# A four-layer transformer kernel, third layer: the mixing step one batch behind instead of two, the gates in one group, unread matmuls in front and beside the first batch

## The reference, cut to what matters

```python
x = x + _L2_xattn_ref(_layernorm(x), ctx, ctx, ...)      # mLSTM
x = x + _L2_ffn_ref(_layernorm(x), W_r, W_k, W_v, mu_r, mu_k)

# mLSTM, per batch and head
gate_input = concat([q, k, v])                # q: normalised x; k, v: ctx
ig, fg = gate_input @ ig_kernel + ig_bias, gate_input @ fg_kernel + fg_bias
cums = cumsum(log_sigmoid(fg))
log_D = cums_i - cums_j + ig_j  (j <= i);  m = max_j log_D;  D = exp(log_D - m)
C = (qh @ kh.T / 8) * D
n = maximum(abs(C.sum(-1)), exp(-m))
h = (C / (n + 1e-6)) @ vh;  h = layernorm(h) * outnorm_weight

# feed-forward
x_prev = x shifted by one token
xr, xk = mu_r * x + (1 - mu_r) * x_prev,  mu_k * x + (1 - mu_k) * x_prev
out = sigmoid(xr @ W_r.T) * (square(relu(xk @ W_k.T)) @ W_v.T)
```

## Time and profile before

| what | us |
| --- | --- |
| median of 3 runs | 1605.3 (1603.09 to 1617.99) |
| the profiled execution, its own time | 1609.19 |
| its span, first to last instruction | 1607.6 |
| the third layer: first DMA issue to last addition | 850.29 to 1091.33 |
| first window's `spread` | 882.15 |
| TensorE busy over the span | 1328.7 (83%) |
| VectorE, ScalarE, GpSimd busy over the span | 808.6, 484.4, 494.1 |

### The profile page before, as it was taken

How to read it: one execution, slowest core, us unless ns; L and a number is a source line. 1 busy time by engine, 2 the same in 40 slices (tenths; PEclk the granted TensorE clock), 3 DMA queues, 4 the chain that set the end, 5 groups by cost and what they waited for, 6 DMA issues and landing times. The chain is left out here.

```text
span 1607.6 us, 30539 instructions
## 1 busy us (share of the span) xinstructions
PE 1328.7 (83%) x9980; PEld 1067.6 (66%) x9980; DVE 808.6 (50%) x2539; ACT 484.4 (30%) x1095; POOL 494.1 (31%) x481
## 2 busy tenths in 40 slices
PE   5988899958888887988974899876889888899991
PEld 4766788945555556887874778754555556788881
DVE  6786334445667643332543455753555655333333
ACT  3554011115554430110111334523455443111010
POOL 1245422231323325223122455542222423211110
PEclk9999899979999988999995557987999999899996
DMA  9001343221013005544433000000000301333216
GB/s 302 1 29 42 125 141 122 70 76 33 29 34 117 29 15 178 171 137 132 133 96 115 14 1 1 1 1 20 14 8 22 105 23 41 111 122 122 82 43 219
DMA packets 87027, 123.58 MB, mean 77 GB/s; under 512 B 11425, under 2 KB 61601, under 8 KB 86657
## 3 DMA queue, kind: packets, MB, share of 16 engines
q1 hardware_dynamic: 49744, 56.10, 11.4%
q10 hardware_dynamic: 25824, 34.10, 6.8%
q0 software_dynamic: 11344, 31.92, 5.5%
HBM read 83.96 MB, written 38.13 MB: 76 GB/s over the span
## 5 line engine op out<-in xcount | busy, mean ns | idle before, releaser
L1243 PEld LDWEIGHTS bank<-f_xT,f_up 128*128 128x128 f32 x2144 | 259.8, 195 | 8.4 <-DVE f_xT L1127 3.1
L1243 PE MATMUL bank<-f_xT,f_up 128*128 128x128 f32 x2144 | 261.0, 278 | 2.1 <-DVE f_xT L1127 2.1
L375 DVE TENSOR_REDUCE mha_nmax<-bank 128x2 f32<-128x512 f32 x256 | 170.3, 687 | 162.4 <-PE bank L496 121.0
L1252 PE MATMUL bank<-f_down,f_hT 128*128 128x256 f32 x832 | 202.2, 386 | 16.7 <-DVE f_hT L1161 16.7
L496 PE MATMUL bank<-l_took,mha_q 32*128 32x256 f32 x1024 | 155.7, 424 | 60.6 <-DVE mha_nmax L375 44.8
L281 ACT ACTIVATE l_took<-bank 128x512 f32<-128x512 f32 x256 | 139.3, 598 | 159.2 <-PE bank L504 140.8
L1252 PEld LDWEIGHTS bank<-f_down,f_hT 128*128 128x128 f32 x832 | 151.7, 192 | 40.3 <-issue 23.0
L496 PEld LDWEIGHTS bank<-l_took,mha_q 32*128 32x128 f32 x1024 | 94.0, 195 | 103.0 <-DVE mha_nmax L375 63.9
L504 PE MATMUL bank<-l_took 32*128 32x256 f32 x1024 | 152.1, 415 | 2.2 <-DVE l_took L384 2.0
L1017 POOL DMA_INDIRECT yout<-f_y,f_to x66 | 63.7, 964 | 287.6 <-DVE f_y L1185 165.9
L1059 ACT ACTIVATE f_hT<-bank,f_b 128x128 f32<-128x128 f32 x148 | 46.4, 364 | 319.2 <-PE bank L1243 319.2
(11 more groups left out here) (287 smaller groups left out, 2441.8 us busy)
## 6 DMA issues: line engine op xcount, KB each, us to landing
f_up<-in_W ACTq DMA_DIRECT2D x26, 512.0 KB, 5.1
f_xt<-rows SPq DMA_DIRECT2D x88, 132.0 KB, 2.1
f_down<-in_W ACTq DMA_DIRECT2D x20, 512.0 KB, 6.1
f_xt<-rows SPq DMA_DIRECT2D x20, 264.0 KB, 2.8
ring<-yout SPq DMA_DIRECT2D x8, 512.0 KB, 4.2
mha_ctxT<-in_ctxT SPq DMA_DIRECT2D x16, 256.0 KB, 2.8
l_took<-yout SPq DMA_DIRECT2D x16, 256.0 KB, 5.5
f_up<-in_W SPq DMA_DIRECT2D x6, 512.0 KB, 7.5
```

What stands on the lines that cost most here:

```text
L375: vector.tensor_reduce(nmax[:, p, :, at], ps_s[n % 2][:, :].rearrange("p (k s) -> p k s", s=S), AX.X, ALU.min).then_inc(max_ready, 1)
L1243: ins = pe.matmul(into, up[q][i][:, c, m * P:(m + 1) * P], xT[:, c, :], start=c == 0, stop=c == DC - 1)
L1252: ins = pe.matmul(ps_y[:, 0:D], hT[:, m, :], down[q][:, m, :], start=m == 0, stop=m == HC - 1)
```

## The change

The mixing chain of a batch now runs wholly in the window after its mLSTM step (LAG = 1), so the loop has 9 windows. `project_k` no longer shares its stretch with `gates`, which are a group of eight at the place where `project_k` stood, ordered by tile of tokens; `turn_f` moves between the values of heads 1 and 2, and the three projections follow the values of heads 2 and 3, with `sum_up` and `turn_g` between them. They write other banks (ps_s[0], ps_s[1], ps_q[0] instead of ps_x, ps_s[0], ps_s[1]). The normalisation `f_normalize` goes from GpSimd to VectorE; GpSimd keeps the root. On VectorE `f_mean_and_var` stands first in the window and `mix` behind the weighing of heads 2 and 3. On ScalarE `f_turned` stands before `softened`, and `squared_relu` and `receptance` behind `squares`. TensorE gets 20 unread matmuls at the start of the layer, and in the first window, which has no mixing work, 4 in the place of each projection.

```diff
+    LAG = 1
-            def f_normalize(b):
+            def f_root(b):
                 pool.wait_ge(f_var_ready, b + 1)
                 pool.tensor_tensor(f_rstd[:, b, :], f_var_eps[:, b, :], G.mhalf(TPB), ALU.pow).then_inc(f_rstd_ready, 1)
-                pool.wait_ge(f_rstd_ready, b + 1)
-                after(pool, fT_done, b)
-                for i in range(TPB):
-                    ins = pool.tensor_scalar(fxn[:, i, :], X[:, TPB * b + i, :], f_moments[:, b, i, 0:1],
-                                             f_rstd[:, b, i:i + 1], ALU.subtract, ALU.mult)
-                ins.then_inc(fxn_ready, 1)
...
+                if w_ >= LAG:
+                    f_turned(w_ - LAG)
                 if more:
                     softened(w_ + 1)
-                if w_ >= 2:
-                    receptance(w_ - 2)
                 if now:
                     squares(w_)
-                if 0 < w_ <= B:
-                    f_turned(w_ - 1)
+                if w_ >= LAG:
+                    squared_relu(w_ - LAG)
+                    receptance(w_ - LAG)
...
+            def f_normalize(b):
+                vector.wait_ge(f_rstd_ready, b + 1)
+                after(vector, fT_done, b)
+                for i in range(TPB):
+                    ins = vector.tensor_scalar(fxn[:, i, :], X[:, TPB * b + i, :], f_moments[:, b, i, 0:1],
+                                             f_rstd[:, b, i:i + 1], ALU.subtract, ALU.mult)
+                ins.then_inc(fxn_ready, 1)
...
+            def fill(w_, n):
+                pe.wait_ge(xnT_ready, min(w_ + 2, B))
+                keep_busy(pe, G, ps_x, n)
...
+            keep_busy(pe, G, ps_s[0], 20)
             centre(0)
             turn_x(0)
...
-            for w_ in range(B + 2):
+            for w_ in range(B + LAG):
...
-                if w_ >= 2:
-                    project_k(w_ - 2, w_ + 1 if more else None)
-                elif more:
+                if more:
                     gates(w_ + 1)
...
+                if w_ >= LAG:
+                    turn_f(w_ - LAG)
                 if now:
                     values(w_, 2)
                     values(w_, 3)
+                if w_ >= LAG:
+                    project_k(w_ - LAG)
+                else:
+                    fill(w_, 4)
+                if more:
+                    sum_up(w_ + 1)
+                if w_ >= LAG:
+                    project_r(w_ - LAG)
+                else:
+                    fill(w_, 4)
                 if more:
                     turn_g(w_ + 1)
-                if w_ >= 2:
-                    project_v(w_ - 2)
+                if w_ >= LAG:
+                    project_v(w_ - LAG)
+                else:
+                    fill(w_, 4)
                 if more:
                     turn_m(w_ + 1)
-                if 0 < w_ <= B:
-                    turn_f(w_ - 1)
                 if w_ + 2 < B:
                     turn_x(w_ + 2)
```

More of the change, by code:

```diff
@@ L2149, in _ @@
             vector.wait_ge(w_in, 16 * 4)
-            for w_ in range(B + 2):
+            for w_ in range(B + LAG):
                 now, more = w_ < B, w_ + 1 < B
+                if w_ >= LAG:
+                    f_mean_and_var(w_ - LAG)
                 if now:
@@ L2162, in _ @@
                     mean_and_var(w_ + 2)
+                if w_ + 3 < B:
+                    z_mean_and_var(w_ + 3)
                 if now:
@@ L2208, in turn_x, with gates @@
                 after(pe, xnT_ready, b)
[L2209 to L2210 removed]
+                after(pe, fT_ready, b - 1 - LAG)
                 turn(xn[:, b % 2, :, :]).then_inc(xT_done, 1)
[L2213 to L2220 removed]
+            def gates(b):
                 pe.wait_ge(xnT_ready, b + 1)
@@ L2223, in await_gates @@
                 after(pe, top_ready, b)
-            def gates(b):
-                await_gates(b)
-                for n in range(2 * TPB * DC):
-                    ins = gate(b, n)
+                for k in range(TPB):
+                    for i, source in ((1, ctxT[:, b, :, :]), (0, xnT[:, b % 2, :, :])):
+                        for c in range(DC):
+                            ins = pe.matmul(ps_g[:, 2 * HEADS * k:2 * HEADS * (k + 1)], source[:, c, k * P:(k + 1) * P],
+                                            gates_w[:, i, c, :], start=i == 1 and c == 0, stop=i == 0 and c == DC - 1)
                 ins.then_inc(gates_done, 1)
@@ L2286, in values, with project_k @@
                 ins.then_inc(pv_done, 1)
+            def fill(w_, n):
+                pe.wait_ge(xnT_ready, min(w_ + 2, B))
+                keep_busy(pe, G, ps_x, n)
             def turn_f(b):
                 pe.wait_ge(fxn_ready, b + 1)
[L2290 removed]
+                pe.wait_ge(xnT_ready, min(b + 2 + LAG, B))
                 after(pe, fT_ready, b)
+                turn(fxn).then_inc(fT_done, 1)
+            def project_k(b):
+                pe.wait_ge(k_mixed, b + 1)
+                pe.wait_ge(decay_ready, HEADS * min(b + 1 + LAG, B))
                 after(pe, relu_s, b)
[L2293 to L2311 removed]
+                for m in range(DC):
+                    for c in range(DC):
+                        ins = pe.matmul(ps_s[0][:, m * S:(m + 1) * S], w[:, 1, c, m * P:(m + 1) * P], mixed[:, 1, c, :],
+                                        start=c == 0, stop=c == DC - 1)
+                ins.then_inc(k_done, 1)
             def project(to, source, i):
@@ L2364, in _ @@
                     values(w_, 1)
-                if w_ >= 2:
-                    project_r(w_ - 2)
-                if more:
-                    sum_up(w_ + 1)
+                if w_ >= LAG:
+                    turn_f(w_ - LAG)
                 if now:
```

76 lines of the change are left out of this document (23 added, 53 removed).

## The result

The changed kernel takes 1596.84 us (median of 20 runs, 1580.58 to 1608.01), the kernel before 1611.68 us beside it (20 runs, 1603.09 to 1629.07). The ratio is 0.9913 with a 95% interval of 0.9889 to 0.9937: faster by about 15 us, a little under the 1% (16 us) that the prediction called the least that can be told from no change; a second comparison, with 0.9931, bears it out. The forecast was 1618 us, that is a little slower, and its range of 1582 to 1652 holds the result; the direction was wrong.

A forecast was written before the change was run, and what follows sets the result against it. TensorE was taken to fill the loop's windows, its clock worth more than any wait. Start -1, first window +4, full windows +15 and end -5 gave +13 on 1609.19, or 1618 us on the median's scale, range 1582 to 1652.

The forecast's parts named there:

- case (a): Clock falls near the gates and rises at the projections in each window; 1618 us, about 1600 to 1638; chance 0.52.
- The price of a full window: Full loop windows: 26.3 us each, mean of full-clock and low-clock prices; 158 for six, +15 against 142.8.
- The walk at full clock: A full window followed along TensorE from spread: 20.4 us, bounds 19.7 and 21.2, against 19.3 before.
- The mean of half and half: Full windows priced as the mean of 20.4 us at full clock and 32.1 at low clock: 26.3 us.
- three signs of being wrong: Clock 1.00 from the first window on, full-clock windows at 19 us or below, or no wait before L2303.
- The base: The six full windows of the kernel before, taken as 142.8 us from one profile.
- The end: From the last batch's norms to the last addition: 24.3 us instead of 29.1, -5, bounds -8 and -1.
- The start: Layer's start with 20 unread matmuls: small matmuls gain from a better clock, -1 us, bounds -3 and +5.
- The first window: 24 unread instructions before the next batch's gate chain lengthen the first window: +4 us, bounds -2 and +8.
- Case (b): Unread matmuls bring full clock into the first window and dense projections hold it: -26, 1579 us; chance 0.20.
- Case (c): Gates' group costs the clock in every window and it is not won back: +51, 1656 us; chance 0.20.
- Case (d): One batch behind buys only the shorter end, loop stays at 142.8 us: -2, 1603 us; chance 0.08.

The follow-up runs named there:

- hold: Changed kernel plus three unread matmuls among the gates of each batch from 2 to 7; 1577.9 us (0.9732), in another comparison 1573.87 us (0.9792).
- wait_fill: Changed kernel plus three unread matmuls per window in front of project_k instead of among the gates; 1591.37 us, ratio 0.9901 to the kernel before.
- lag2: Changed kernel with LAG = 2, its orders and banks kept but the mixing chain two windows behind; 1611.37 us, ratio 1.0011 to the kernel before.
- no_front: Changed kernel without the 20 unread matmuls at the start of the layer; ratio 0.9923 to the kernel before.
- pool_norm: Changed kernel with the normalisation for the mixing back on GpSimd; ratio 0.9939 to the kernel before.
- hold_all: hold plus unread matmuls among the gates of batch 1 and 11 and 5 around turn_f in the last window; 1574.19 us, ratio 0.9794.

## Why the prediction was wrong, and where it held

**What bounds the loop, and case (a): right.** Case (a) was that the clock falls at the gates and rises at the projections in each window. The changed kernel does this in every full window, and `hold` and `wait_fill`, with the same three matmuls at two places, show that it is lost in the stretch that begins with the gates.

**The price of a full window: the first step that failed.** It was a plain mean of two prices, 20.4 and 32.1, so 26.3 us. It is 24.0 in the mean of the six, 23.7 to 23.8 in the four in the middle.
- The walk at full clock was too long. From `turn_f` to `project_k` I had 4.3 us (2.82 to the first mixing operation and 1.5 for the two of k); `hold` has 955.40 - 952.38 = 3.0, of which the two of k are 0.89. The waits I put at about 2 and 1 us were 1.13 and 0.53. `hold`'s window of 20.08 us contains 1.5 us of unread matmuls, so without them some 18.6 is my estimate for the price that I had put at 20.4. The 1.5 for k rested on a wrong reading of the 4.59 us in the earlier trace rows: what GpSimd ran beside those four operations were its additions to X (the last row there), not the `normalize` that I expected beside the new ones. In `hold` the two of k ran beside just that `normalize` and took 0.89, while its own two operations took 2.95 us instead of 2.43.
- The mean of half and half had no row behind it. Priced piece by piece from `hold`: from the second pair's `spread` to the end of `project_k` it is 957.23 - 948.65 = 8.6 us, of which 7.5 are work; at the low clock such work takes 1.8 to 1.9 times as long (2.82 / 1.55, 3.78 / 1.99), so 13.6 to 14.2. The rest of the window, less the unread matmuls, is 20.08 - 8.6 - 1.5 = 10.0. Together 23.6 to 24.2, which is what was measured. The wait for the mixing drops out at the low clock, since the values last long enough for k to be mixed when TensorE gets there; I had added 1.4 for it. Its absence before L2303 was one of my three signs of being wrong, and it came.

For six windows that makes +1.2 instead of +15 on the scale of the first profile, a miss of 14 us.

**The base: the second step that failed.** The 142.8 us of the earlier trace rows were taken for the kernel before, and half of its six profiles have 153 to 163. The full clock in three of the windows belongs to three of six executions, not to the kernel. Against the mean of six, 150.4, the same term is -6, another 7 us. So this one term is some 21 us off, 14 by the price and 7 by the base, of the 28 between the forecast's +13 and the measured -15; some 4 more are the end, and the last 3 lie outside what the profiles of the layer show. (The median of three runs that the forecast was set on, 1605.3, was also 6 us under that of twenty.)

**The end: right.** -5 was predicted from the norms of the last batch on, 29.1 to 24.3; it is 23.6, so -5.5. Two or three microseconds more came ahead of the norms, from the last window's first `spread` to the norms, which the walk didn't count (36.52 - 23.6 = 12.9, against 1062.25 - 1047.01 = 15.2 before). That the end depends on the distance of one batch, `lag2` shows. The normalisation took 0.73 us, not the 1.5 allowed for.

**The start: right.** -1 was predicted; -1.8 came between the first two profiles and -1.1 against `no_front`, both no more than the scatter of the starts of the kernel before, 30.1 to 32.0.

**The first window: right in price.** +4 predicted, +2.9 in the first pair of profiles and +4.5 in the means. What it buys, 2.5 us in the second window (27.33 to 24.78), had not been asked for.

**The rivals.** Case (b), the full clock held by the dense projections, didn't happen; that its 1579 us is the time of `hold` is luck, since `hold` had to add work for it, which its shorter windows paid. The Trainium skill's rule in "TensorE: Matmul & The Clock Gate", section "HAM oscillation — how this bites in real kernels", that long idle waits between bursts drop the clock, does not cover this case: the changed kernel's last full window (1015.79 to 1040.05) has TensorE busy for 24.26 of 24.26 us at a granted clock of 0.65. Case (c) is refuted: no full window came near 32 us. (Its sum left out the start's -1.) Case (d), that only the shorter end is left (1603), was nearest in time, and had 0.08. That is luck: its loop in sum is the first profile's, but because the window's price came out in the middle, not because nothing changed. The chances went wrong with the price: with 23.8 us per window instead of 26.3 the centre of (a) is 1603 on the forecast's own scale, and the mass that lay above it would have lain around "no change" and faster.

## What to carry to other kernels

Price a stretch with a changing clock piece by piece: each piece at the clock that its place in the order will see, and a wait only where the other engines' work still sticks out at that clock. Before a change is held against one profile, look whether the kernel gives the same row of window times in several; one that doesn't is better compared by the means of several profiles. Where TensorE loses its clock at one thin group, that is one of matmuls with few columns, a few unread matmuls inside that group can pay (1.5 us of them made a window 4.0 us shorter here), while the same ones a few microseconds later, or in an order with a second thin place, brought nothing.

## What I had not expected of the hardware

- TensorE's clock fell with the engine fully busy: in the changed kernel's last full window behind a group of gates of 8 columns each, with 24.26 of 24.26 us busy and a granted clock of 0.65.
- Executions of one program fall into rows of window times that repeat to 0.1 us, and yet there are several such rows: 142.7, 142.7 and 142.8 us for three of them, 152.9 to 163.3 for three others.
- The clock's pattern can hide an edit of a microsecond or two in a single profile: in `pool_norm` it gave back the 1.7 us that the edit cost, in `hold_all` it took 3 us where the edit brought 2.
- The gates in one group cost the clock where the chain is one batch behind, and yet grouping them in the order of the kernel before helps (1597.99 us); there the clock is back right behind `project_k` in one piece. How these two are weighed in general, and how often the kernel before runs in each of its rows, stays open.
